# Loading the first eight groups' expert outputs ahead of the last four block stores in a mixture-of-experts kernel

## The reference

```python
x = x + _L0_xattn_ref(_layernorm(x), ctx_1024, ctx_1024, mask_BxS2_bk0, ...)
x = x + _L0_ffn_ref(_layernorm(x), ...)
...
g = jax.nn.gelu(xt @ wg1 + bg1, approximate=False)
probs = jax.nn.softmax(g @ wg2, axis=-1)
top_vals, top_idx = jax.lax.top_k(probs, 2)
gates = jnp.zeros_like(probs).at[jnp.arange(n)[:, None], top_idx].set(top_vals)
h = jax.nn.gelu(jnp.einsum('nd,edh->enh', xt, w_in), approximate=False)
o = jnp.einsum('enh,ehd->end', h, w_out)
y = jnp.einsum('ne,end->nd', gates, o)
```

## Time and profile before

| | us |
|---|---|
| median of 3 runs | 765.07 |
| lowest and highest | 763.24, 767.15 |
| the profiled execution's own time | 765.94 |
| its span, first to last instruction | 763.8 |
| last block's result written (end of `yb`) | 722.9 |
| first gather starts | 725.39 |
| last gather starts | 756.20 |
| last add starts | 760.73 |

### The profile page before, as it was taken

How to read it: one execution, slowest core, us unless ns; L and a number is a source line. 1 busy time by engine, 2 the same in 40 slices (tenths; PEclk the granted TensorE clock), 3 DMA queues, 4 the chain that set the end, 5 groups by cost and what they waited for, 6 DMA issues and landing times.

```text
span 763.8 us, 14153 instructions
## 1 busy us (share of the span) xinstructions
PE 574.9 (75%) x4326; PEld 405.7 (53%) x4326; DVE 443.1 (58%) x1706; ACT 407.7 (53%) x862; POOL 359.7 (47%) x438
## 2 busy tenths in 40 slices
PE   3499999889888988898898767483778866789800
PEld 1156666556455555555465446362667755679700
DVE  4267788778777877777785773251323322223374
ACT  2257988887787888688786655230322322224300
POOL 4122126644554564455435326647555555550075
PEclk9989999999999999999998987867898999989955
DMA  3363111221122122201111224324544444446498
GB/s 89 71 195 84 45 41 44 61 67 43 50 60 66 29 65 63 66 24 30 38 29 32 83 59 122 105 77 112 158 133 124 118 125 124 120 131 186 133 364 291
DMA packets 74458, 73.59 MB, mean 96 GB/s; under 512 B 22032, under 2 KB 61840, under 8 KB 74096
## 3 DMA queue, kind: packets, MB, share of 16 engines
q1 hardware_dynamic: 64160, 53.86, 26.8%
q0 software_dynamic: 8640, 18.37, 6.8%
q10 hardware_dynamic: 1584, 0.46, 0.2%
HBM read 44.99 MB, written 27.70 MB: 95 GB/s over the span
## 4 chain that ended last, share of the span: by engine, by line
PE 53%; ACT 14%; issue 13%; DVE 7%; another core or an unknown queue 4%; POOL 4%; SPq 2%; DMA 2%; ACTq 0%; POOLq 0%; DVEq 0%
PE bank L638 12%; PE bank L649 10%; PE bank L462 6%; PE bank L484 6%; DVE sm L890 3%; PE bank L466 3%; POOL gathered L1417 3%; PE bank L475 3%; PE bank L629 3%; ACT sm L717 2%; ACT pt L782 2%; ACT vx L709 2%; ACT rows L744 2%; PE bank L491 2%
## 5 line engine op out<-in xcount | busy, mean ns | idle before, releaser
L1354 POOL DMA_INDIRECT routed_rows<-rows,pos x128 | 125.2, 978 | 136.4 <-ACT rows L746 86.2
L1390 POOL DMA_INDIRECT expert_rows_by_token<-yb,token_row x118 | 113.2, 960 | 85.7 <-DVE token_row L1248 40.8
L638 PE MATMUL bank<-xbT,wi 128*128 128x256 f32 x312 | 97.1, 439 | 71.1 <-issue 70.4
L827 ACT ACTIVATE hb<-bank 128x512 f32<-128x512 f32 x78 | 46.6, 597 | 168.7 <-PE bank L638 77.4
L1254 DVE TENSOR_TENSOR yb<-bank,gate 128x256 f32<-128x256 f32 x78 | 33.1, 424 | 172.2 <-PE bank L649 107.2
L638 PEld LDWEIGHTS bank<-xbT,wi 128*128 128x128 f32 x312 | 59.6, 212 | 84.7 <-issue 77.0
L882 DVE TENSOR_REDUCE smax<-bank 128x8 f32<-128x512 f32 x128 | 82.2, 683 | 30.7 <-PE bank L466 25.4
L649 PE MATMUL bank<-wo,hb 128*128 x624 | 91.6, 295 | 0.0
L649 PEld LDWEIGHTS bank<-wo,hb 128*128 128x128 f32 x624 | 85.3, 212 | 0.1
L462 PE MATMUL bank<-kx,qT 64*64 64x512 f32 x512 | 74.6, 654 | 14.0 <-DMA kx<-kT 7.1
L890 DVE TENSOR_TENSOR sm<-bank,smax 128x512 f32<-128x512 f32 x128 | 81.9, 681 | 0.0
(11 more groups left out here) (135 smaller groups left out, 934.8 us busy)
## 6 DMA issues: line engine op xcount, KB each, us to landing
xb<-routed_rows SPq DMA_DIRECT2D x78, 138.0 KB
wi<-w_in SPq DMA_DIRECT2D x78, 128.0 KB
kx<-expert_rows_by_token SPq DMA_DIRECT2D x26, 256.0 KB
ctx_in<-ctx_t SPq DMA_DIRECT2D x16, 256.0 KB
x_all<-x SPq DMA_DIRECT2D x16, 256.0 KB
kx<-kT SPq DMA_DIRECT2D x256, 16.0 KB
out<-x_all SPq DMA_DIRECT2D x16, 256.0 KB
expert_rows<-yb SPq DMA_DIRECT2D x19, 128.0 KB, 2.1
```

The costliest lines, as they stand in the source:

```text
L638: last = nc.tensor.matmul(UBK[b % 2][:, c * BLK:(c + 1) * BLK], wi[:, b % RX, c * P:(c + 1) * P], xbT[:, b % RH, :], start=True, stop=True)
L1354: nc.gpsimd.indirect_dma_start(out=rows_d, out_offset=bass.IndirectOffsetOnAxis(ap=pos[:, buf, k, u:u + 1], axis=0), in_=rows[:, buf, u, : ...
L1390: nc.gpsimd.indirect_dma_start(out=tok_d, out_offset=bass.IndirectOffsetOnAxis(ap=token_row[:, b % RY, u:u + 1], axis=0), in_=yb[:, b % RY ...
```

## The change

The wait for the part-one scatters and the loads of lots 0 to 7 are moved in SP's program, from behind the loop over the groups to the end of the turn in which the group number is the number of groups less three, which is group 24. They then stand behind the stores of blocks 71 to 73 and ahead of those of blocks 74 to 77, that is of the last two groups. No instruction is added or taken away, on any engine.

```diff
@@ -408,10 +408,11 @@
                     if p == PARTS - 1:
                         for b in range(first, first + n):
                             store_block(b)
-                for i in range(RY):
-                    sp.wait_ge(s_ysc[i], 16 * BT * len(range(i, NBS[0], RY)))
-                for q in range(RL):
-                    load_expert_rows(q)
+                    if g == len(GROUPS) - 3:
+                        for i in range(RY):
+                            sp.wait_ge(s_ysc[i], 16 * BT * len(range(i, NBS[0], RY)))
+                        for q in range(RL):
+                            load_expert_rows(q)
                 for q in range(SPS[0]):
                     sp.wait_ge(s_sum, q + 1)
                     store_tiles(q * U)
```

## The result

The changed kernel takes 768.27 us (median of 18 runs, 764.37 to 770.51) where the kernel before, run beside it, takes 763.23 us (18 runs, 757.2 to 768.89). The ratio is 1.0071, with a 95% interval from 1.0047 to 1.0094: 0.7% slower. By the medians that is 5.0 us, by the ratio 5.4; the ratio is of means and leaves out one slow run of the kernel before, the 768.89, which is over 1.5% above its fastest. The profiled execution has a span of 768.2 us, before 763.8.

What follows compares the result with a forecast made beforehand. Bound: the end chain of PE's matmuls, last store's landing, POOL's gathers and adds. 761.6 + 3.0 + 0.6 + 2.8 = 768.0 us span against 763.8, + 4.2; on the 765.07 median, 769.3 us, range 766.2 to 772.6.

Steps and rivals of the forecast that it cites:

- Start of the loads: SP's first moved load, behind block 73's store: starts at 716.8 us, 7.1 us earlier than before.
- rival (d): A wait on the scatters holds SP until the old time, so the change does nothing: 765.1 us, chance 0.02.
- SP's order: SP issues 16 loads before the last four stores: last store issued at 726.5 instead of 722.9, 3.6 us late.
- The queue: Stores on SP's queue wait until the loads are through: last store lands at 731.6 us, 7.0 us later.
- rival (a): Stores aren't held by the queue and only SP's issuing order costs: 765.7 us, chance 0.12.
- The row of gathers: POOL's 24 gathers, first start to last start: 29.3 us instead of 30.81, 1.5 us won.
- the jam: Full DMA engines behind the first load, 370 GB/s at a share of 1.10 from 737 to 759 us.
- The last landing: Landing of POOL's last gather: 3.0 us instead of 4.18, 1.2 us won.
- The tail: After the last gather lands: unchanged, 0.6 us of adds and 2.8 us for the last out store.
- Won back in all: From first gather to end of span (Y): 1.5 us in the gathers' steps plus 1.2 us in the last landing.
- Rival (b): Gathers keep their 30.8 us and 4.18 us, so nothing is won back: 772.1 us, chance 0.15.
- PE under the loads: PE at blocks 74 to 77 while the moved loads run: costed at nothing, last matmul stays at 722.4 us.

Runs made afterwards that it cites:

- e1: Changed kernel with each of the 16 moved loads carrying a quarter of its bytes; 655.89 us, ratio to the kernel before 1.0128.
- e4: Changed kernel with waits and loads one group later, ahead of block 77's store alone; 660.33 us, ratio to the kernel before 1.0202.
- e9: Second run of the changed kernel with quarter-size moved loads; 656.23 us, ratio to the kernel before 1.0122.
- e11: Second run of the changed kernel with the loads ahead of block 77's store alone; 660.76 us, ratio to the kernel before 1.0194.
- e12: Changed kernel with only four lots ahead of the stores of blocks 74 to 77, four behind them; 656.78 us, ratio to the kernel before 1.0129.
- the repeat: The changed kernel unaltered, run again in another set; 768.36 us, ratio to the kernel before 1.0071.
- e7: Kernel before with waits behind group 21's stores and lots 0 to 7 loaded in pairs behind groups 21 to 24; 764.97 us, ratio 1.0039.

## Why the prediction was right

The forecast was 769.3 us, 0.55% slower; measured are 768.27 us and 0.71%. The forecast stood on a kernel before of 765.07 us, which measured 763.23 beside the change. That the two times lie 1.0 us apart says little, then; the loss itself came out 0.8 to 1.2 us above the 4.2 foretold. Point by point, with times counted from the last `yb`, since PE came there 0.9 us earlier in the profiled execution:

- **Start of the loads.** Foretold 5.7 us ahead of the last `yb` (716.8 and 722.48); 715.90 and 721.60 are 5.7. The waits cost nothing there. This held only because the scatters had ended, and it was partly luck that they had: rival (d) had no weight in this trace, and where the scatters end late, its wait is real and costs more than the change itself (e1, e4, e9, e11, e12). I read the 29 us of slack as a property of the kernel, while it was one of the chip that the trace came from.
- **SP's order.** The last store issued 4.0 us after the start of the last `yb` (726.5 and 722.48); measured 725.41 - 721.60 = 3.8, before 0.45. Counted by the store's issue, this is 3.4 us of the loss.
- **The queue.** Landing foretold 9.1 us after the last `yb`; measured 9.6 (731.16 and 721.60). From issue to landing it is 5.75 us instead of 1.68, the other 4.1 us of the loss. With a quarter of the bytes it is 1.9 us (e1, e9), but that alone would also fit a store slowed by full engines. The DMA packets of after decide it. A load's packets are of 2 KB, a store's of 1 KB, the semaphores' under 512 B; the stretches are 723.9 to 728.5 us and 728.5 to 731.2:

```profile
DMA packets 982, 1.79 MB, mean 389 GB/s; under 512 B 108, under 2 KB 108, under 8 KB 982
DMA packets 1188, 1.01 MB, mean 374 GB/s; under 512 B 94, under 2 KB 1066, under 8 KB 1188
```

In the first stretch the four stores are issued, and not one packet between 512 B and 2 KB moves: all 1.79 MB are the loads'. In the second there are 972 such packets, the four stores' 512 and the first of the out store behind them. So the stores stand in line behind the loads, and rival (a), a queue that doesn't hold the store, falls. The lots' order of landing had foretold it. It also follows that 3.4 and 4.1 us aren't two separate prices: the first of the stores was issued at 723.98 and moved nothing before 728.5 either, so by these packets an earlier issue at the same place in the queue would have gained nothing.
- **The row of gathers.** Foretold 29.3 us from first start to last start, measured 761.86 - 731.93 = 29.9 (30.6 in the repeat). Of the 2.0 us of long steps I kept 0.5, and it was 1.1. This term was mis-sized, because I laid all long steps to the jam. The row at 747.43 above takes 1.44 us at a DMA share of 0.45 and 111 GB/s, and with quarter loads in the old order the row took 30.9 us. What makes them long isn't shown, but the traces point at DVE rather than the jam. Of the 336 gathers in the 14 traces, 105 take over 1.00 us, and DVE is at work during a part of every one of them; the 68 that meet no instruction of DVE's take 0.99 us at most, in the jam too. In after DVE stands still during the first six gathers, as it had added its first five lots before them. The other 163 also lie beside DVE's work and stay at 1.00 us or less, and no run took DVE's adds away, so this is a rival cause left to test.
- **The last landing.** 2.50 us (2.57 in the repeat), foretold 3.0.
- **The tail** of adds and the last out store: 768.2 - 764.36 = 3.8 us, taken as 3.4.
- **Won back in all**: Y fell by 2.1 us (1.4 in the repeat), foretold 2.7. Rival (b), nothing won back, is half refuted: the row of gathers hardly gains, the landing does.
- **PE under the loads**: no gap; the last three `yb` are at the same distances as before. Loads ahead of PE's own rows are another thing (e7).

The sum foretold was + 4.2 us. Measured it is + 5.3: 0.5 more at the landing, 0.6 more in the row of gathers, 0.4 more in the tail, 0.5 less at the last landing. The Trainium skill, "DMA: Bandwidth & Descriptors", section "Queues, rings and completion order", has an engine take up descriptors in ring order; this case's runs agree, with the packets above and the 5.75, 6.50 and 6.80 us of the held stores (after, e11, e4). It also says that completion isn't FIFO per issuing engine; no run here shows the last store, the one that the gathers wait for, landing ahead of its loads.

## What to carry to other kernels

Before a transfer is moved ahead into idle room, look at what stands behind it on the same queue: it pays for their issues or for their bytes, whichever lasts longer (the issues with the quarter loads, the bytes with the whole ones), and what counts is what is left of both when the transfer that the chain waits for is ready, not how many transfers are passed. A part of the work small enough to be through by then is free; the rest belongs behind it. And a wait moved with the work is free only by the slack that its releaser has, so ask whether that slack is the kernel's or only that of the execution that you look at.

## What the runs showed of the hardware

- **A gather of 64 KB lands late when the DMA engines are full, on a queue of its own too.** In after the first tile's gathers start at 731.93 and 733.23, and DVE can add it only at 739.18, 5.9 us after the second one's start; the last gather, in quiet, lands in 2.50 us. From 731.9 to 736.7 us, with four gathers started, the profile has packets of SP's queue (q1) alone and none of POOL's (q0):

```profile
q1 hardware_dynamic: 1897, 1.83, 108.4%
```

So much of the delay lies ahead of a gather's first packet. Whether a store on ACT's queue would wait as long isn't shown.
- **Issuing from SP isn't small beside the transfer.** Back to back, a store or load takes SP about 0.47 us, 16 small ones 7.43 us, which is 141 GB/s for transfers of 64 KB.
- **The same program took 762 to 765 us on some chips and 648 us on others.** The stretch of the experts shows the difference. Before, then the kernel with ACT's stores (columns as above):

```profile
480.00:680.00 200.00, 136.02 (x777) 118.71 (x777) 60.72 (x329) 51.44 (x112) 118.28 (x124) 0.86 0.43 122
...
440.00:600.00 160.00, 155.33 (x1044) 139.58 (x1042) 75.47 (x390) 66.94 (x150) 120.95 (x127) 0.99 0.66 193
```

PE is busy for 68% of the one stretch and for 97% of the other, and its gaps in the former (64.0 us in 27 of them at L638, the longest 10.4) are put down to "issue", that is to nothing that the profile shows. Their cause stays open. A change of some microseconds at the end has to be judged beside a kernel before on the same chip.
